# Weighted sums in pairs of chunks, the last 26 queries over four key quarters at once, plain turns of the output

## The reference

```python
top_u = max(1, L // TOP_FACTOR)                       # 2048 // 5 = 409
_, top_idx = jax.lax.top_k(norm(Q), top_u)
scores = einsum("bud,bld->bul", Q_sel, K) / hd ** 0.5
out_sel = einsum("bul,bld->bud", softmax(scores), V)
out = zeros.at[top_idx].set(out_sel)                  # the other rows stay zero
x = x + ga * (out @ Wo.T + bo)                        # after an adaptive layer norm
x = x + gb * ffn(layernorm(x) * (1 + cb) + sb)        # 512 -> 1408 -> 512, quantised to fp4 in blocks of 16
```

## Time and profile before

| what | value |
|---|---|
| median of 3 runs | 3646.24 us (3642.79 to 3647.29) |
| the profiled execution | 3647.05 us, its span 3645.2 us |
| busy in the span | PE 91%, DVE 76%, POOL 41%, ACT 28% |
| costliest groups of `attend` | DVE L1038 x512: 618.5 us; ACT L1117 x512: 483.0 us; PE L1208 x2048: 453.0 us |

### The profile page before, as it was taken

The page is one execution under the profiler, slowest core; times in us unless marked ns, Lnnn a source line. Parts: engine busy times, 40 slices in busy tenths (PEclk is TensorE's granted clock), DMA queues, the critical chain, the costliest instruction groups (busy, mean ns, idle before and its releaser), DMA issues. The chain is left out here.

```text
span 3645.2 us, 50953 instructions
## 1 busy us (share of the span) xinstructions
PE 3308.7 (91%) x16784; PEld 1498.4 (41%) x16784; DVE 2764.1 (76%) x3797; ACT 1035.5 (28%) x1454; POOL 1512.2 (41%) x1311
## 2 busy tenths in 40 slices
PE   5999997036999999999986999999999999999998
PEld 2554553021323332333323555555555555555554
DVE  4677675975666666666645898989898989898986
ACT  1332331003555555555541111111111111111111
POOL 0332331004555555555533444444444444445442
PEclk8999998567999999999997999999999999999999
DMA  5656556102222222222212100010101010101000
GB/s 185 180 181 208 177 176 196 44 1 66 68 73 72 72 73 68 73 67 74 72 41 81 32 30 32 29 32 29 32 29 32 29 32 29 32 29 32 29 23 15
DMA packets 194398, 252.71 MB, mean 69 GB/s; under 512 B 58581, under 2 KB 114261, under 8 KB 193493
## 3 DMA queue, kind: packets, MB, share of 16 engines
q1 hardware_dynamic: 177944, 245.07, 21.6%
q0 software_dynamic: 16384, 6.76, 1.2%
HBM read 154.68 MB, written 97.04 MB: 69 GB/s over the span
## 5 line engine op out<-in xcount | busy, mean ns | idle before, releaser
L1038 DVE TENSOR_REDUCE top<-ps_max 128x1 f32<-128x1024 f32 (+1 forms) x512 | 618.5, 1219 | 340.9 <-PE ps_max L1171 340.8
L1117 ACT ACTIVATE p<-ps_exp,p_bias 128x820 f32<-128x820 f32 x512 | 483.0, 943 | 457.6 <-PE ps_exp L1197 457.6
L1208 PE MATMUL ps_out<-p,v_tok 128*33 128x410 f32 x2048 | 453.0, 521 | 0.0
L1007 POOL DMA_INDIRECT o_d<-o_rows,chosen x256 | 249.0, 973 | 446.6 <-DVE o_rows L1064 373.7
L1642 ACT ACTIVATE silu<-f_g 128x512 f32<-128x512 f32 (+1 forms) x192 | 107.8, 561 | 801.5 <-PE f_u L1711 801.5
L1171 PE MATMUL ps_max<-k_max,q_max 96*128 96x512 f16 (+1 forms) x1024 | 314.4, 389 | 1.1 <-DVE top L1038 0.8
L1197 PE MATMUL ps_exp<-q_exp,k_exp 98*128 98x410 f16 x1024 | 266.7, 342 | 44.7 <-ACT p L1117 44.7
L1711 PE MATMUL f_g<-gu,xT_lo 128*128 128x512 f16 (+1 forms) x768 | 278.3, 362 | 0.0
L1709 PE MATMUL f_g<-gu,xT_hi 128*128 128x512 f16 (+1 forms) x768 | 278.1, 362 | 0.0
L1710 PE MATMUL f_g<-gu,xT_hi 128*128 128x512 f16 (+1 forms) x768 | 278.1, 362 | 0.0
L1709 PE MATMUL f_u<-gu,xT_hi 128*128 128x512 f16 (+1 forms) x768 | 277.5, 361 | 0.0
(11 more groups left out here) (201 smaller groups left out, 6417.7 us busy)
## 6 DMA issues: line engine op xcount, KB each, us to landing
k_max<-k_d SPq DMA_DIRECT2D x192, 128.0 KB
k_exp<-k_d SPq DMA_DIRECT2D x192, 128.0 KB
v_d<-v SPq DMA_DIRECT2D x16, 1056.0 KB, 7.5
v_tok<-v_d SPq DMA_DIRECT2D x64, 264.0 KB, 2.9
x<-in_x SPq DMA_DIRECT2D x16, 1024.0 KB, 6.5
q_d<-q SPq DMA_DIRECT2D x16, 1024.0 KB, 6.5
o_d<-zeros SPq DMA_DIRECT2D x16, 1024.0 KB, 8.5
a_in<-o_d SPq DMA_DIRECT2D x64, 256.0 KB, 2.6
```

The lines of the kernel that those rows point to most:

```text
L1007: pool.indirect_dma_start(o_rows, bass.IndirectOffsetOnAxis(ap=con["chosen"][0:n, t, h:h + 1], axis=0), o_rows_of[u][0:n, t, :], None).the ...
L1038: ve.tensor_reduce(top[0:rows_of(t), t, half:half + 1], ps_max[c % 2][0:rows_of(t), :, :].rearrange("p a n -> p (a n)"), AX.X, ALU.max, ne ...
L1117: act.activation(p32[k % PB][:, :, :], ps_exp[:, :, 0:NQ], ACT.Exp, bias=con["p_bias"][:, 0:1], scale=scale).then_inc(p_done, 1)
L1208: last = pe.matmul(ps_out[at:at + VCOLS, 0:NQ], v_tok[u][:, t, :], p32[k % PB][:, s, :], start=k == 0, stop=k == STEPS - 1)
```

## The change

It does four things, all in `attend`:

1. `weigh` runs at the odd steps alone, on two chunks one behind the other: at k = 1 the chunks 6 and 7 of head i-1, at k = 3, 5 and 7 the chunks 0 and 1, 2 and 3, 4 and 5 of head i.
2. The two chunks of the 26 queries become one: four matmuls of 26 queries by 512 keys, one for each quarter of the keys, into the partitions from 0, 32, 64 and 96 of one bank. CH is 7. One reduction over 512 columns takes their maxima (`top_last`). To bring the four of a query together, DVE multiplies `top_last` with `group` (128 x 4), PE multiplies the result with `same_row` into `ps_misc` (`gather_last`), and `top_rows` reduces those four numbers.
3. `turn_output` uses four transposes with the identity, which leave the halves apart (97 columns a tile); `divide` copies the odd halves out of `ps_misc`, adds the even ones, and then takes reciprocal and product.
4. The steps have new work: k = 0 `turn_queries` and two chunks of maxima; k = 2 two chunks (the small one among them); k = 4 `gather_last` and two chunks; k = 6 one chunk and `rows`; k = 5 `turn_output` ahead of `weigh`. ACT's `take_queries`, `take_output` and `take_top` come behind the exponentials of k = 0, 2 and 6. DVE has `queries_again` at k = 2, `top_rows` at k = 4, and `divide` between the two chunks of k = 4. Three chunks (EARLY) of a head are done two slots ahead, where there were two.

The diff, cut to its core:

```diff
-    CH = 2 * QT
+    FULL = 2 * (QT - 1)
+    CH = FULL + 1
     HALF = L // 2
-    EARLY = 2
-    LAG = 3
-    QUERIES_AT = 3
-    OUT_AT = LAG
+    QUARTER = L // 4
+    EARLY = 3
+    QUERIES_AT = 0
+    OUT_AT = 2
+    GATHER_AT = 4
     TURN_AT = 5
+    ROWS_AT = 6
+    CHUNKS_AT = {0: ((1, 3), (1, 4)), 2: ((1, 5), (1, 6)), 4: ((2, 0), (2, 1)), 6: ((2, 2),)}
...
+    ve.memset(top1[:, :], 0.0).then_inc(top_zero, 1)
+    ident = con["ident"][:, :].rearrange("p (j r) -> p j r", r=HD)
+    ve.tensor_reduce(group[:, :], ident, AX.X, ALU.add).then_inc(groups_set, 1)
+    ve.tensor_reduce(same_row[:, :], con["ident"][:, :].rearrange("p (j r) -> p r j", r=HD), AX.X, ALU.add)\
+      .then_inc(groups_set, 1)
     ve.wait_ge(top_zero, 1)
...
-    def max_chunk(h, c):
+    ve.wait_ge(groups_set, 2)
+
+    def max_chunk(h, u, c):
         t, half = c // 2, c % 2
         ve.wait_ge(max_ready, h * CH + c + 1)
-        ve.tensor_reduce(top[0:rows_of(t), t, half:half + 1],
-                         ps_max[c % 2][0:rows_of(t), :, :].rearrange("p a n -> p (a n)"), AX.X, ALU.max,
-                         negate=True).then_inc(max_done, 1)
+        ps = ps_max[(u + c) % 2]
+        if c < FULL:
+            ve.tensor_reduce(top[:, t, half:half + 1], ps[:, :, :].rearrange("p a n -> p (a n)"), AX.X, ALU.max,
+                             negate=True).then_inc(max_done, 1)
+        else:
+            ve.tensor_reduce(top_last[:, :], ps[:, 0, :], AX.X, ALU.max, negate=True).then_inc(max_done, 1)
+            ve.wait_ge(max_done, h * CH + CH)
+            need(ve, top_gathered, h)
+            ve.tensor_scalar(by_group[:, :], group[:, :], top_last[:, 0:1], None, ALU.mult).then_inc(group_step, 1)
     def top_rows(h):
-        ve.wait_ge(max_done, h * CH + CH)
-        ve.tensor_reduce(top1[:, :], top[:, :, :], AX.X, ALU.min).then_inc(top_step, 1)
-        ve.wait_ge(top_step, h * 2 + 1)
+        ve.tensor_reduce(top1[:, 0:QT - 1], top[:, :, :], AX.X, ALU.min).then_inc(top_step, 1)
+        ve.wait_ge(top_gathered, h + 1)
+        ve.tensor_reduce(top1[0:Q_LAST, QT - 1:QT], ps_misc[0:Q_LAST, 0:4], AX.X, ALU.min).then_inc(top_step, 1)
+        ve.wait_ge(top_step, h * 3 + 2)
         need(ve, rows_ready, h)
         ve.tensor_copy(top_parts[:, :, 0], top1[:, :]).then_inc(top_step, 1)
-        ve.wait_ge(top_step, h * 2 + 2)
+        ve.wait_ge(top_step, h * 3 + 3)
         ve.tensor_tensor(top_parts[:, :, 1], top1[:, :], top_parts[:, :, 0], ALU.subtract).then_inc(top_done, 1)
...
         ve.wait_ge(o_turned, h + 1)
-        sums = ps_misc[:, 0:QT * VCOLS].rearrange("p (t r) -> p t r", r=VCOLS)
-        ve.reciprocal(o_inv[:, :], sums[:, :, HD]).then_inc(o_inverse, 1)
-        ve.wait_ge(o_inverse, h + 1)
+        turned = ps_misc[:, 0:QT * OROWS].rearrange("p (t r) -> p t r", r=OROWS)
+        ve.tensor_copy(o_odd[:, :, :], turned[:, :, VTILE:OROWS]).then_inc(o_step, 1)
+        ve.wait_ge(o_step, h * 3 + 1)
+        ve.tensor_tensor(o_both[:, :, :], turned[:, :, 0:VCOLS], o_odd[:, :, :], ALU.add).then_inc(o_step, 1)
+        ve.wait_ge(o_step, h * 3 + 2)
+        ve.reciprocal(o_inv[:, :], o_both[:, :, HD]).then_inc(o_step, 1)
+        ve.wait_ge(o_step, h * 3 + 3)
         need(ve, o_stored[u], stored)
-        ve.tensor_tensor(o_rows_of[u][:, :, :], sums[:, :, 0:HD],
+        ve.tensor_tensor(o_rows_of[u][:, :, :], o_both[:, :, 0:HD],
                          o_inv[:, :].unsqueeze(2).to_broadcast([P, QT, HD]), ALU.mult).then_inc(o_divided, 1)
...
     def slot(i, u):
         for k in range(STEPS):
-            d, c = chunk_of(k)
-            if has(i, d):
-                max_chunk(i + d, c)
-            if k == 0 and has(i, 1):
+            if k == GATHER_AT and has(i, 1):
+                top_rows(i + 1)
+            for n, (d, c) in enumerate(CHUNKS_AT.get(k, ())):
+                if n == 1 and k == GATHER_AT and has(i, -1):
+                    divide(i - 1, 1 - u, stored_before(i, u, -1))
+                if has(i, d):
+                    max_chunk(i + d, (u + d) % 2, c)
+            if k == OUT_AT and has(i, 1):
                 queries_again(i + 1, 1 - u)
-            if c == CH - 1 and has(i, 1):
-                top_rows(i + 1)
-            if k == TURN_AT and has(i, -1):
-                divide(i - 1, 1 - u, stored_before(i, u, -1))
...
     def slot(i, u):
         for k in range(STEPS):
-            if k == OUT_AT and has(i, -1):
-                take_output(i - 1)
             exponentials(i, k)
             if k == QUERIES_AT and has(i, 2):
                 take_queries(i + 2, u)
-            if k == STEPS - 1 and has(i, 1):
+            if k == OUT_AT and has(i, -1):
+                take_output(i - 1)
+            if k == ROWS_AT and has(i, 1):
                 take_top(i + 1, 1 - u)
...
-        for s in range(2):
-            at = half * HALF + s * 512
-            last = pe.matmul(ps_max[c % 2][0:rows_of(t), s, :], q_max[u][:, t * P:t * P + rows_of(t)],
-                             k_max[u][:, at:at + 512], start=True, stop=True)
+        ps = ps_max[(u + c) % 2]
+        if c < FULL:
+            for s in range(2):
+                at = half * HALF + s * 512
+                last = pe.matmul(ps[:, s, :], q_max[u][:, t * P:(t + 1) * P], k_max[u][:, at:at + 512],
+                                 start=True, stop=True)
+        else:
+            for j in range(4):
+                last = pe.matmul(ps[j * HD:j * HD + Q_LAST, 0, :], q_max[u][:, t * P:NQ],
+                                 k_max[u][:, j * QUARTER:(j + 1) * QUARTER], start=True, stop=True)
         last.then_inc(max_ready, 1)
+    def gather_last(h):
+        pe.wait_ge(group_step, h + 1)
+        if isinstance(h, int):
+            pe.wait_ge(qsel_done, min(h + 2, BH))
+            if h == BH - 1:
+                pe.wait_ge(rows_done, h)
+        else:
+            pe.wait_ge(qsel_done, h + 2)
+        pe.matmul(ps_misc[0:HD, 0:4], same_row[:, :], by_group[:, :], start=True, stop=True).then_inc(top_gathered, 1)
...
-    def turn_output(h, queries):
+    def turn_output(h):
         pe.wait_ge(o_done, h + 1)
-        if queries is not None:
-            pe.wait_ge(qsel_done, queries)
-        elif h < BH - 1:
-            pe.wait_ge(rows_done, h + 2)
+        if isinstance(h, int) and h >= BH - 2:
+            pe.wait_ge(o_divided if h == BH - 1 else rows_done, h if h == BH - 1 else BH)
         else:
-            pe.wait_ge(o_divided, h)
+            pe.wait_ge(top_step, h * 3 + 8)
         for t in range(QT):
-            last = pe.matmul(ps_misc[:, t * VCOLS:(t + 1) * VCOLS], o32[:, t * P:(t + 1) * P], fold[:, :],
-                             start=True, stop=True)
+            last = pe.transpose(ps_misc[:, t * OROWS:(t + 1) * OROWS], o32[:, t * P:(t + 1) * P],
+                                con["ident"][0:OROWS, 0:OROWS])
...
     def slot(i, u):
         for k in range(STEPS):
-            d, c = chunk_of(k)
-
-            if k == 0 and has(i, -1):
-                weigh(i - 1, 1 - u, STEPS - LAG, None)
             scores(i, u, k, in_turn(i, u, 0))
-
-            if k == LAG and has(i, d):
-                scores_for_max(i + d, (u + d) % 2, c, in_turn(i, u, d))
+            if k == TURN_AT and has(i, -1):
+                turn_output(i - 1)
+            if k == 1 and has(i, -1):
+                for c in (STEPS - 2, STEPS - 1):
+                    weigh(i - 1, 1 - u, c, None)
+            elif k > 1 and k % 2 == 1:
+                for c in (k - 3, k - 2):
+                    weigh(i, u, c, in_turn(i, u, 0))
             if k == QUERIES_AT and has(i, 2):
                 turn_queries(i + 2, u)
-            if k >= LAG:
-                weigh(i, u, k - LAG, in_turn(i, u, 0))
-            elif k > 0 and has(i, -1):
-                weigh(i - 1, 1 - u, STEPS + k - LAG, None)
-            if k == TURN_AT and has(i, -1):
-                turn_output(i - 1, i + 3 if has(i, 2) else None)
-            if k == STEPS - 1 and has(i, 1):
+            if k == GATHER_AT and has(i, 1):
+                gather_last(i + 1)
+            for d, c in CHUNKS_AT.get(k, ()):
+                if has(i, d):
+                    scores_for_max(i + d, (u + d) % 2, c, in_turn(i, u, d))
+            if k == ROWS_AT and has(i, 1):
                 rows(i + 1)
-            if k != LAG and has(i, d):
-                scores_for_max(i + d, (u + d) % 2, c, in_turn(i, u, d))
```

More of the change, by code:

```diff
@@ L240, in project @@
         f_ps = m.ps("f_ps", [P, N])
-        ve_held, pool_held, act_held, sp_held = (keep.sem(f"p1_{e}_held") for e in ("ve", "pool", "act", "sp"))
+        ve_held, pool_held, act_held, sp_held = (con["held"][e] for e in ("ve", "pool", "act", "sp"))
         bias_loaded = keep.sem("bias_loaded")
@@ L880, in attend @@
         q_exp = [m.sb(f"q_exp{u}", [KROWS + 2, NQ], F16) for u in range(2)]
-        top = m.sb("top", [P, QT, 2], F32)
+        top = m.sb("top", [P, QT - 1, 2], F32)
+        top_last = m.sb("top_last", [P, 1], F32)
+        by_group = m.sb("by_group", [P, 4], F32)
```

(38 more changed lines are left out.)

13 lines of the change are left out of this document (7 added, 6 removed).

## The result

The changed kernel takes 3537.83 us (median of 4 runs, 3534.74 to 3538.50) against 3645.20 of the kernel before on the same chip. The ratio is 0.9704, 95% interval 0.9687 to 0.9721, so it is faster by 107 us. The forecast was 3551, a gain of 95. A later job on another chip, where the kernel before took 3655, has the changed kernel at 3582 and a ratio of 0.9801 (0.9788 to 0.9815): there the gain is 73 us, short of the forecast.

The account below looks back on a forecast made before the run. PE bounds `attend`, each step costing the larger of 1.64 us and its PE work. Slots fall from 16.33 to 14.76 us: 62 x 1.57 = 97, less 1 for the ends, from 3647.05 gives 3551 us; range 3537 to 3618.

Parts of the forecast that it names:

- Pairs: Odd steps: scores 0.45, first chunk of `weigh` 0.81, second 0.68, together 1.94 us.
- rival of exposed weight loads: `weigh` in the loop: record pairs pay their weight loads; 55 us more where only the second chunk pays, 3606; chance 0.04.
- the rule beside it: Skill page: weight loads overlap matmuls in flight only if row groups differ, so each pair of `weigh` records would wait.
- The small chunk: 26 queries at k = 2: four matmuls fully overlapped cost PE 0.42 us, without overlap 1.08.
- Gather: `gather_last` at k = 4: two records of an f32 matmul, taken at 0.3 us, ends 0.1 to 0.5.
- Turn: `turn_output` at k = 5: four f32 transposes at 0.44 us replace 1.01, making the step 2.38.
- The chain: Scores, exponentials, scores over the single `ps_exp`: no step shorter than 1.64 us, which all four even steps cost.
- Margins: Slack before PE waits: 0.1 us at `weigh` of k = 3, 0.9 at the gather, 1.0 at `rows`.
- rivals of thin margins: Even steps outgrow the chain, or `weigh` of k = 3 waits for `take_output`: about 0.5 us a slot, 3582; chance 0.19.
- of the gather: At k = 4 PE stands before `gather_last`, waiting for DVE's product: 74 us slower, 3721; chance 0.06.
- that of slower: Kernel gets slower, by PE waiting at k = 4 for DVE's product: 3721 us; chance 0.06.
- the first rival: Even steps outgrow the chain and thin margins at k = 3: about 0.5 us a slot, 31 us, 3582; chance 0.19.

Follow-up runs that it names:

- Experiments 1: Changed kernel with one chunk of weighted sums at k = 0, 1, 4, 5, 6 and 7, none at 2, a pair at 3: 3597.5 us.
- 2: Kernel before with only the pairs of chunks at the odd steps, nothing else moved: 3769.6 us, ratio 1.0345.
- 7: Changed kernel with `turn_output` moved to k = 4, chunk (2,1) to k = 6 and `rows` ahead of the chunks there: 3563.9 us, ratio 0.9751.
- experiment 3: Changed kernel with the 26 queries in two chunks again and no gather: 3580.7 us, ratio 0.9822.
- experiment 6: Changed kernel with ACT's exponential waiting first for the free buffer, then for the scores: 3583.1 us, ratio 0.9796.

## Why the prediction was right

*The bound.* A step costs the larger of the chain over `ps_exp` and PE's own work. Experiments 1, 2 and 7 show it from both sides. A chunk of weighted sums put into k = 0, which was full, costs 0.93 us (1.64 to 2.57). Taken out of the even steps 2, 4 and 6 of the kernel before, it gives back only what stood above the chain: 1.70, 1.80 and 1.71 us become 1.63, 1.56 and 1.56. The turn put into k = 4, which had room, costs that step nothing where no exponential is late, and k = 5 falls by 0.34.

*Pairs.* Forecast 1.94 for an odd step, measured 1.96. The second chunk costs 0.69 as in the earlier trace rows, in the loop too. The rival of exposed weight loads, and the rule beside it, fall.

*The small chunk.* Taken at 0.42 for full overlap, and the four matmuls do overlap. It hardly matters: at k = 2 PE waits 0.35 us for the exponential anyway. Its worth is 15 us (experiment 3) and comes from where the room is and from DVE's shorter work, not from PE's 0.6 us. How the 15 us divide between PE and DVE was not tested.

*Gather.* Taken at 0.3, measured 0.16; the scores ahead of it cost 0.45 and not the 0.35 of the sum. Together 0.04 less, in a step that ends with the chain: no effect.

*Turn.* Taken at 0.44 with k = 5 at 2.38, measured 0.43 and 2.29: the scores ahead of it cost 0.36 and not 0.45, and `weigh` behind it pays its change within the 0.43. I had counted that change twice, 0.09 x 62 = 6 us.

*The chain.* Taken at 1.64 in all even steps, from one row. It is 1.63 at k = 2 and 1.56 at k = 4 and 6 (at k = 0 PE's own work is 1.64), for a reason that experiment 6 shows: at k = 0 to 2 the loop waits for the scores in a register instruction ahead of the exponential, and ACT starts 0.08 us later. 2 x 0.08 x 56 = 9 us. This and the turn are the terms mis-sized. Together they are 15 us, and the forecast was short of the gain by 12; the odd steps k = 1, 3 and 7, at 1.96 and not 1.94, take back 3 x 0.02 x 56, about 3 us.

*The waits.* Forecast about 70 us of waiting for the exponentials, at the even steps; measured 43.6, in the steady slots at k = 2 and 6 alone. The even steps have more work on PE than the sum gave them: k = 2 has 1.63 - 0.35 = 1.28 against 1.20, k = 6 has 1.56 - 0.24 = 1.32 against 1.14, and k = 0 none left over. As all stay at or below the chain, the time does not feel it. The sign of eight records of `weigh` in about 2.0 us contradicts the prediction's own 0.81 + 0.68; it is 1.57.

*Margins.* None was used up in the first profile: `weigh` of k = 3 did not wait for `take_output`, nor `gather_last` for DVE. The rivals of thin margins and of the gather fall, and so does that of slower.

*What the forecast had no term for* is how late an exponential can come in a loop. In the later job the changed kernel is at 3582 us against 3538 and the kernel before at 3655 against 3645, so the gain is 73 us and not 107. In the profiles, `attend` is 49 us longer from the first scores to the last. Before, ACT's exponential was on the path once a slot; in the changed kernel it is on it, or within 0.1 us of it, in the four even steps, and each lateness there falls on the total. That the forecast came within 12 us is in this sense luck of the job: in the later one the gain is 73 us where 95 were forecast, and its 3582 us are the number of the first rival by chance, since no even step outgrew the chain by its work on PE, and of the margins PE waited 8 times for DVE, 1.5 us in all. Even in the first job the time is only 1 us above the low end of the range (3537), and below the forecast's own range of 3540 to 3570.

## What to carry to other kernels

Where a chain through one buffer sets a floor for each step, PE work is only worth saving in steps above that floor: sum step by step and move work from full steps into those with room; saving alone, as the pairs did, can cost. Group f32 products of narrow column groups behind each other: the second chunk costs 0.69 us and the first 0.81, plus 0.10 for the scores ahead of it. And once a chain between two engines sets most steps, run the same kernel in more than one job, and try the loop written out: here that took the time from about 3564 to 3521 us, though in different jobs.

## What the runs showed of the hardware

- The raise of a semaphore by PE was recorded up to 1.8 us behind the modelled end of its product. ACT's exponentials came 0.3 to 1.5 us late at fixed places of the loop, in single slots up to 2.3, in one job and not in another for the same kernel (slots of 15.3 and 14.54 us), 98 of 107 of them right behind a late raise; DVE was late in the same steps (0.91 against 0.26 us). Written out, in another job, one exponential was late.
- How soon an exponential follows its scores depends on which instruction does the waiting: 0.037 us for its own, 0.097 for a semaphore instruction ahead of it, 0.115 for a register instruction ahead of it.
- Four matmuls of 26 columns by 512 into four groups of partitions start within 0.01 us, in a row of 0.40 us where one alone is 0.39.
- f32 transposes of 97 x 128 follow each other on PE at 0.08 to 0.09 us (128 x 128: 0.11), f32 products of 97*128 with 33 columns, of two records each, at 0.22.
